# Exponential in PSUM with its shift as a bias, and the last v product ahead of the transposes

## The reference, cut to what matters

```python
# layer 0
q = einsum('c,bcn->bn', wq, x); k = einsum('c,bcn->bn', wk, x)
s = q[:, None, :] + k[:, :, None]
att = softmax(where(s > 0, s, 0.01 * s), axis=-1)
agg = einsum('bcn,bmn->bcm', x, att)
h = layernorm(x + relu(einsum('oc,bcm->bom', adj, agg) + bm))
# layer 1
z_l = h @ W_lang.T; z_g = h @ W_grav.T; v = h @ W_V.T
zn = z_l / max(norm(z_l), EPS)
A_l = max(zn @ zn.T, 0) * not_eye
d2 = max(sq + sq.T - 2 * z_g @ z_g.T, 0)          # sq = sum(z_g * z_g)
A_g = exp(-d2 / (2 * sigma * sigma)) * not_eye
K_l = row_stochastic(A_l * adj); K_g = row_stochastic(A_g * adj)
K = w * K_l + (1 - w) * K_g
out = layernorm(h + (K @ v) @ W_O.T)
```

## Time and profile before

| | us |
|---|---|
| runs | 1106.06, 1103.53, 1105.68 |
| median | 1105.68 |
| the profiled execution, its own time | 1105.26 |
| its span, first to last instruction | 1103.3 |
| PE busy | 1051.6 (95%) |
| DVE busy | 921.5 (84%) |
| ACT busy | 621.2 (56%) |
| POOL busy | 325.9 (30%) |
| mean granted share of TensorE's clock | 0.996 |

### The profile page before, as it was taken

How to read it: one execution, slowest core, us unless ns; L and a number is a source line. 1 busy time by engine, 2 the same in 40 slices (tenths; PEclk the granted TensorE clock), 3 DMA queues, 4 the chain that set the end, 5 groups by cost and what they waited for, 6 DMA issues and landing times. The chain is left out here.

```text
span 1103.3 us, 20017 instructions
## 1 busy us (share of the span) xinstructions
PE 1051.6 (95%) x7429; PEld 721.2 (65%) x7429; DVE 921.5 (84%) x2474; ACT 621.2 (56%) x1171; POOL 325.9 (30%) x280
## 2 busy tenths in 40 slices
PE   7989999999999999999999999999999999999995
PEld 4466766576666666766676676667667666766663
DVE  5767888988888898988888898898888889888867
ACT  2557466474746647465564756556475664747331
POOL 0333323142431414233141333305143231514100
PEclk9999999999999999999999999999999999999998
DMA  7020020030301103030110203002030200301011
GB/s 273 14 77 1 1 94 23 1 116 1 115 2 77 40 1 116 1 115 1 68 49 1 115 1 116 1 33 84 1 115 1 110 7 4 112 1 77 1 40 38
DMA packets 22833, 56.33 MB, mean 51 GB/s; under 512 B 1744, under 2 KB 2256, under 8 KB 20688
## 3 DMA queue, kind: packets, MB, share of 16 engines
q1 hardware_dynamic: 22736, 55.06, 13.6%
HBM read 21.50 MB, written 16.78 MB: 35 GB/s over the span
## 5 line engine op out<-in xcount | busy, mean ns | idle before, releaser
L1103 POOL TENSOR_TENSOR att_lo<-att,att_hi 128x512 f16<-128x512 f32 x128 | 157.0, 1238 | 218.1 <-ACT att_hi L531 218.1
L849 DVE SCALAR_TENSOR_TENSOR att<-a_row,u_col,vb 128x512 f32<-128x512 f32 x128 | 126.9, 1011 | 29.7 <-POOL att_lo L1103 29.7
L220 PE MATMUL bank<-xw_hi,att_hi 128*128 128x257 f16 x512 | 140.4, 274 | 1.2 <-DVE wvo_lo L739 1.0
L572 ACT ACTIVATE z_hi<-bank 128x512 f16<-128x512 f32 x128 | 75.6, 590 | 117.2 <-PE bank L222 116.4
L221 PE MATMUL bank<-ht_lo,z_hi 128*128 128x256 f16 x512 | 139.6, 273 | 0.0
L220 PE MATMUL bank<-ht_hi,z_hi 128*128 128x256 f16 x512 | 139.6, 273 | 0.0
L222 PE MATMUL bank<-ht_hi,z_lo 128*128 128x256 f16 x512 | 139.6, 273 | 0.0
L222 PE MATMUL bank<-xw_hi,att_lo 128*128 128x257 f16 x512 | 139.5, 272 | 0.0
L221 PE MATMUL bank<-xw_lo,att_hi 128*128 128x257 f16 x512 | 139.1, 272 | 0.0
L856 DVE TENSOR_TENSOR z_lo<-bank,z_hi 128x512 f16<-128x512 f32 x128 | 87.4, 688 | 39.8 <-ACT z_hi L572 37.7
L606 ACT ACTIVATE agg_t<-bank,den_inv 128x256 f32<-128x256 f32 x128 | 58.3, 472 | 89.8 <-DVE den_inv L788 89.8
(11 more groups left out here) (173 smaller groups left out, 2765.6 us busy)
## 6 DMA issues: line engine op xcount, KB each, us to landing
x_in<-in_x SPq DMA_DIRECT2D x16, 1024.0 KB, 5.3
x_res<-x_in SPq DMA_DIRECT2D x16, 1024.0 KB, 5.3
out_y<-o SPq DMA_DIRECT2D x32, 512.0 KB, 3.2
agg_t<-in_wl SPq DMA_DIRECT2D x4, 256.0 KB, 3.6
y<-in_wg SPq DMA_DIRECT2D x1, 1024.0 KB, 9.7
o<-in_wv SPq DMA_DIRECT2D x1, 1024.0 KB, 11.9
h<-in_woT SPq DMA_DIRECT2D x1, 1024.0 KB, 14.0
att<-in_adjT SPq DMA_DIRECT2D x1, 256.0 KB, 3.8
```

The source lines that it names most:

```text
L220: pe.matmul(dst, ah, bh, start=(i == 0 and first), stop=False, skip_group_check=skip)
L572: act.activation(z_hi[:, g, :], bank[g % 4][:], ACT.Copy).then_inc(s["z_hi_done"], 1)
L849: dve.scalar_tensor_tensor(out=att[:, g % 2, :], in0=a_row[:, j, :], scalar=u_col[:, j, n:n + 1], in1=vb[:, g % 2, :], op0=ALU.mult, op1=A ...
L1103: pool.tensor_tensor(att_lo[:, n[0], n[1], :], att[:, g % 2, :], att_hi[:, n[0], n[1], :], ALU.subtract).then_inc(s["att_lo_done"], 1)
```

## The change

The gravity exponential is computed by ACT in PSUM, in place, one instruction for each half bank (128 x 256), with the row's shift as its bias. The shift has to be multiplied by the same coefficient c_grav first: neg_gs, two small DVE instructions a step. The clamp before the exponential is replaced by a bound on its result: DVE's masked multiply now reads PSUM, takes min(value, 1) and multiplies by the mask, with the row sums as before, and stands where the clamps stood. c_grav is bounded at 1e30. On ACT the exponentials of a full step go ahead of v_hi(2), and v_hi(3) goes from behind the relus to ahead of kt_hi. On PE v product 3 goes ahead of the transposes L419 and L428 and waits for ag_done, since bank 7 holds the second gravity kernel until the masked multiply has read it; in the last step it goes into bank 0. On DVE v_lo(3) goes from before the last statistic to behind the first one.

```diff
-        v_bank = (0, 1, 2, 7)
+        def v_banks(l0):
+            return [bank[i] for i in ((0, 1, 2, 7) if l0 else (0, 1, 2, 0))]
...
-                def last_v():
-                    pe.wait_ge(s["clamp_done"], 2 * p + 2)
+                if l1:
+                    if l0:
+                        pe.wait_ge(s["ag_done"], 2 * p + 2)
+                    else:
+                        pe.wait_ge(s["v_lo_done"], 4 * p + 1)
                     v_product(3)
-
-                if l1 and not l0:
-                    last_v()
-                if l1:
 
                     for j in range(2):
                         pe.wait_ge(s["k_done"], 2 * p + j + 1)
...
-                if l1 and l0:
-                    last_v()
                 if l1:
 
                     for k in range(4):
...
-                    for k in range(3 if l0 else 1):
+                    for k in range(2 if l0 else 1):
                         v_hi_tile(k)
                     for j in range(2):
 
-                        act.wait_ge(s["clamp_done"], 2 * p + j + 1)
-                        act.activation(a_g[:, j], a_g[:, j], ACT.Exp, scale=c_grav[:, 0:1]).then_inc(s["exp_done"], 1)
+                        act.wait_ge(s["s_mm"], 4 * p + 3 + j)
+                        act.wait_ge(s["neg_gs_done"], 2 * p + j + 1)
+                        for c in range(OC):
+                            last = act.activation(halves[6 + j][:, c, :], halves[6 + j][:, c, :], ACT.Exp,
+                                                  bias=neg_gs[:, 2 * j + c:2 * j + c + 1], scale=c_grav[:, 0:1])
+                        last.then_inc(s["exp_done"], 1)
+                    if l0:
+                        v_hi_tile(2)
...
                     v_hi_tile(2)
+                if l1:
                     v_hi_tile(3)
-                if l1:
                     for j in range(2):
                         act.wait_ge(s["kt_mm"], 2 * p + j + 1)
...
-                if l1 and l0:
-                    v_hi_tile(3)
...
+                def neg_gs_tile(j):
+
+                    dve.wait_ge(s["neg_g_done"], 2 * p + j + 1)
+                    dve.tensor_scalar(neg_gs[:, 2 * j:2 * j + 2], neg_g[:, 2 * j:2 * j + 2], c_grav[:, 0:1], None,
+                                      ALU.mult).then_inc(s["neg_gs_done"], 1)
...
+                    if l1 and g == 12:
+                        wait(dve, s["exp_done"], 2 * p)
+                        neg_gs_tile(0)
...
                         t_lo_tile(k)
+                    neg_gs_tile(1)
                     v_lo_tile(0)
                     if l0:
                         v_lo_tile(1)
                     for j in range(2):
-
-                        dve.wait_ge(s["s_mm"], 4 * p + 3 + j)
-                        dve.wait_ge(s["neg_g_done"], 2 * p + j + 1)
+                        dve.wait_ge(s["exp_done"], 2 * p + j + 1)
                         for c in range(OC):
-                            last = dve.tensor_scalar(a_g[:, j, c, :], halves[6 + j][:, c, :],
-                                                     neg_g[:, 2 * j + c:2 * j + c + 1], 0.0, ALU.add, ALU.min)
-                        last.then_inc(s["clamp_done"], 1)
+                            k = 2 * j + c
+                            last = dve.scalar_tensor_tensor(out=a_g[:, j, c, :], in0=halves[6 + j][:, c, :], scalar=1.0,
+                                                            in1=mask[:, c, :], op0=ALU.min, op1=ALU.mult,
+                                                            accum_out=deg_g[:, k:k + 1])
+                        last.then_inc(s["ag_done"], 1)
...
-                    for k in range(4):
-
-                        j, c = k // 2, k % 2
-                        dve.wait_ge(s["exp_done"], 2 * p + j + 1)
-                        last = dve.scalar_tensor_tensor(out=a_g[:, j, c, :], in0=a_g[:, j, c, :], scalar=1.0,
-                                                        in1=mask[:, c, :], op0=ALU.mult, op1=ALU.mult,
-                                                        accum_out=deg_g[:, k:k + 1])
-                    last.then_inc(s["ag_done"], 1)
...
                         y_stat_tile(k)
+                        if l1 and k == 0:
+                            v_lo_tile(3)
                     y_stat_tile(1)
...
-                    if l1:
-                        v_lo_tile(3)
                     y_stat_tile(3)
```

More of the change, by code:

```diff
@@ L124, in build @@
         sq_l, sq_lc, r_l = sb("sq_l", [4]), sb("sq_lc", [4]), sb("r_l", [4])
-        neg_g = sb("neg_g", [4])
+        neg_g, neg_gs = sb("neg_g", [4]), sb("neg_gs", [4])
         a_l, a_g = sb("a_l", [2, OC, O]), sb("a_g", [2, OC, O])
@@ L159, in build @@
             t_hi_done t_lo_done s_mm sq_l_done sq_lc_done r_l_done neg_g_done shift_done
-            clamp_done exp_done v_mm v_hi_done v_lo_done r_mm mr_done al_done dl_done sl_done ag_done
+            neg_gs_done exp_done v_mm v_hi_done v_lo_done r_mm mr_done al_done dl_done sl_done ag_done
             dgr_done sg_done kl_done k_done kt_mm kt_hi_done kt_lo_done o_mm o_done o_stat_done
@@ L356, in v_product @@
                         rows = slice(k * P, (k + 1) * P)
-                        pe_last = product(bank[v_bank[k]][:], [(ht_hi[:, d, rows], ht_lo[:, d, rows],
+                        pe_last = product(v_banks(l0)[k][:], [(ht_hi[:, d, rows], ht_lo[:, d, rows],
                                                         wvo_hi[:, d, :], wvo_lo[:, d, :]) for d in range(DC)])
@@ L565, in v_hi_tile @@
                     act.wait_ge(s["v_mm"], 4 * p + k + 1)
-                    act.activation(v_hi[:, k, :], bank[v_bank[k]][:], ACT.Copy).then_inc(s["v_hi_done"], 1)
+                    act.activation(v_hi[:, k, :], v_banks(l0)[k][:], ACT.Copy).then_inc(s["v_hi_done"], 1)
                 for g in range(8 + 6):
@@ L752, in constants @@
                 dve.tensor_scalar(c_out[:], unscale[:, 4:5], 1.0 / 256.0, None, ALU.mult)
-                dve.tensor_scalar(c_grav[:], tiny[:, 1:2], unscale[:, 3:4], None, ALU.mult)
+                dve.tensor_scalar(c_grav[:], tiny[:, 1:2], unscale[:, 3:4], 1e30, ALU.mult, ALU.min)
                 dve.tensor_scalar(tiny[:, 6:7], scale[:, 2:3], NORM_EPS2, None, ALU.mult).then_inc(s["coef_done"], 1)
@@ L792, in v_lo_tile @@
                     dve.wait_ge(s["v_hi_done"], 4 * p + k + 1)
-                    dve.tensor_tensor(v_lo[:, k, :], bank[v_bank[k]][:], v_hi[:, k, :], ALU.subtract)\
+                    dve.tensor_tensor(v_lo[:, k, :], v_banks(l0)[k][:], v_hi[:, k, :], ALU.subtract)\
                        .then_inc(s["v_lo_done"], 1)
@@ L953, in step @@
                     dve.tensor_tensor(deg_l2[:], deg_l[:], r_l[:], ALU.mult).then_inc(s["dl_done"], 1)
-                    dve.wait_ge(s["ag_done"], p + 1)
+                    dve.wait_ge(s["ag_done"], 2 * p + 2)
                     dve.tensor_scalar(deg_g2[:], deg_g[:], DEG_EPS, None, ALU.max).then_inc(s["dgr_done"], 1)
```

## The result

The changed kernel takes 1117.93 us (median of 4 runs, 1116.56 to 1119.58) against 1105.65 before: ratio 1.0112, 95% interval 1.0094 to 1.0131. The prediction was 1115.7, slower. The profiled execution took 1116.56, with a span of 1114.7.

What follows compares the result with a forecast made beforehand. PE, 95% busy, was taken as the bound, so only its idle time could move. 8.7 for middle steps + 2.0 - 0.7 = +10.0 us on the median 1105.68 gave 1115.7 us; 8 in 10 range 1106 to 1134.

Steps and rivals of the forecast that it cites:

- The stall goes: PE around transposes L419 and L428, waiting for a_l and agg_t: 1.17 us of stall per step disappears.
- The relu is 1.35 late: ACT, middle step: kt_hi and relus queue behind the later transposes, so the first relu starts 1.35 us late.
- v_lo(3) gives back 0.48: DVE: v_lo(3) moved behind the first y_stat returns 0.48 of the 1.35 us.
- h 0.87 late, PE +0.62 a step: Middle steps: last y_stat and h 0.87 us late, slack 0.25, so PE loses 0.62 in each of 14 steps: +8.7.
- The exponentials are free up to 0.76 each: ACT: four 128x256 exponentials fit the 3.06 us idle before v_hi(2), costing nothing up to 0.76 us each.
- DVE's shortening counts 0: DVE gets some 3.3 us a step shorter, only before a_l, where PE no longer waits: 0.
- Last step but one, +2.0: Last pair but one: L419 never stalled, PE already waits 2.23 for h, and y comes later: +2.0 us.
- Last pair, -0.7: Last step: four multiplies leave DVE's queue before kt_lo, masks wait for the exponentials: -0.7 us, between 0 and -1.7.
- The clock, taken as 0: After PE's longer idle before h in the last step but one, a clock fall would add 1.7 us; taken as 0.
- The port: Rival: POOL's second y add gets in before DVE's; 15 x 1.17 = 17.6 us more, 1133.3 us; chance 0.17.
- The y path was not hidden: Refers to the faster rival: relus, adds and h stay within the slack, 1088.6 us; chance 0.14.

Runs made afterwards that it cites:

- vlo_late: The changed kernel with DVE's v_lo(3) back in its old place before the last y statistic; 1126.01 us, ratio 1.0182.
- order_alone: The kernel before with only the new order of v product 3, v_hi(3) and v_lo(3), exponential part as before; 1117.73 us, ratio 1.0114.
- exp_alone: The changed kernel without its new order: v product 3, v_hi(3) and v_lo(3) in their old places; 1089.21 us, ratio 0.9852.
- half_v: exp_alone with two of v product 3's four terms ahead of the kernel matrix's transposes, two behind agg_t's; 1105.83 us, ratio 0.9999.
- addt_late: exp_alone with PE's last transposed addition behind v product 2 instead of ahead of it; 1072.61 us, ratio 0.9692.
- hold_alone: The kernel before with ACT writing the exponential to PSUM and DVE's masked multiply reading it there, at its old place; 1091.14 us, ratio 0.9860.
- sbuf_early: exp_alone with the exponential written to SBUF and the masked multiply reading it there, at the early place; 1091.10 us, ratio 0.9858.

## Why the prediction was right, step by step

- *The stall goes.* Right: 1.17 a step, in the change and by either part alone.
- *The relu is 1.35 late, v_lo(3) gives back 0.48.* Right: 1.35 measured, and 0.51 by vlo_late.
- *h 0.87 late, PE +0.62 a step.* Measured 0.83 and, from step to step, 65.69 - 65.06 = 0.63. The new waits, 1.79 in all, were put before the x products and L478; they are there, 1.84 from start to start.
- *The exponentials are free up to 0.76 each.* Right: 0.549 in the mean (the nearest row had 0.464), and ACT still idled 1.26 before v_hi(2).
- *DVE's shortening counts 0.* Right for this change, as order_alone shows, but only beside the new order. This is the gap in the reasoning that a right total hides: the prediction knew the 2.33 us multiply, and that it stood before a_l, for which PE waits, and gave each part no price alone. The exponential part alone took 1089.2 (exp_alone).
- *Last step but one, +2.0.* Right: L478 waits 4.34 instead of 2.23 and starts at 14.90 instead of 12.90.
- *Last pair, -0.7.* Mis-sized: 0.26, from 3.30 to 3.04 between the end of the v products and the o products. The four multiplies left DVE's queue, but they freed only some 1.4 us of it (0.35 from start to start), and the masks stood there 1.04 us for the exponentials, a wait that the prediction gave no figure. The last a_l ended 0.60 after the v products instead of 0.85. The wait for kt_lo is 1.74 as before.
- *The clock, taken as 0.* Mis-sized, and the largest error: 2.2 us in the profiled execution, see below; the prediction had named 1.7 as its price if it fell. With 2.2 the sum would have been 12.2, where the medians differ by 12.3. That they agree so closely is in part luck: with the last pair put right too it would be 12.6, and the medians need not hold the clock's 2.2 in full: the kernel before was profiled in an execution with a mean granted clock of 0.996, while most of its others beside the experiments show 0.994, so some of those probably lost clock too. No profile of them shows where.
- *The rivals.* The port went the way of the sum: DVE's second y addition took 0.68, in all 14 steps alike, with a lead of 0.06 us, as close as foreseen. What a later start would have cost was not tried. The y path was not hidden.

## What to carry to other kernels

On an engine that is nearly full, moving independent work ahead of a short wait is paid by whatever stands behind it: look up first how much slack the longest path out of the passed instructions has (0.25 us here), since a wait that doesn't appear in the table may be that near. Before covering a stall, look at what ends it: here it was one instruction of 2.33 us that ought to take 0.41, and removing its cause brought 1.4% where covering it cost 1.1%. When two parts of a change aim at one stall, time each alone.

## What the runs showed of the hardware

A long wait of PE can cost its clock as well. In the change PE idles 4.34 us before L478 of the last step but one. The stretches before and behind it (PEclk is the third column from the end):

```profile
1052.00:1056.60 4.60, 0.34 (x2) 0.00 (x0) 4.48 (x8) 0.00 (x0) 1.22 (x2) 0.81 0.00 0
1056.70:1061.50 4.80, 4.80 (x20) 3.91 (x21) 2.55 (x4) 2.39 (x4) 0.00 (x0) 0.50 0.01 3
```

and the transposes of h there, beside 1.97 us in the earlier trace rows:

```profile
1056.68 3.68 PE L478 MATMUL bank<-ident,h 128*128 128x128 f32 x16 [4.34 <-DVE h L1054]
```

The granted clock was 0.50 there, the 1.2 GHz level. These transposes and the z products behind them, the first few of which still ran at 0.50, take 3.47 + 13.72 us instead of 2.07 + 12.96 (from start to start): 2.2 us lost after the wait itself. In the profiles of order_alone, half_v and vlo_late, with waits of 4.3, 3.0 and 3.0 us there, the clock fell as well. With 2.2 us it stayed up before, in exp_alone and in addt_late, and fell for 3.4 us in hold_alone and sbuf_early. What decides between these is not shown.

A masked multiply on DVE with two SBUF sources stands still while POOL's x_lo runs (2.33 us), a multiplication of four columns does so too (1.02 instead of 0.14), and with one source in PSUM the multiply does not (0.40 to 0.42). The Trainium skill, "SBUF — State Buffer", section "SBUF: two separate sides", says that a DVE operation with two SBUF inputs and a GpSimd operation that reads SBUF lock each other out for a whole instruction. The traces agree.
